# Stacking hi and lo query features in one 128-row operand, and both heads' probabilities through one set of value weights, in the first attention of a two-layer kernel

## The reference, cut to what matters

```python
c_q = hidden_states @ w_q_down                      # 192 latent features
q_nope = c_q @ w_q_up_nope ; q_rope = rope(c_q @ w_q_up_rope)
c_kv = hidden_states @ w_kv_down                    # 64 latents, shared by all heads
q_lat = einsum('bhsd,hdr->bhsr', q_nope, wuk)       # 64 wide
scores = (q_lat . c_kv + q_rope . k_rope) / sqrt(192), causal mask
probs = softmax(scores)
out_lat = einsum('bhst,btr->bhsr', probs, c_kv)     # 64 wide per head
out = einsum('bhsr,hdr->bhsd', out_lat, wuv) ; return out @ w_out
```

## Time and profile before

| | |
|---|---|
| time, median of 3 runs | 2554.64 us (2553.92 to 2555.03) |
| the profiled execution | 2551.88 us, span 2550.0 us |
| PE busy | 2338.2 us, 92% of the span |
| DVE, ACT, POOL busy | 69%, 57%, 62% |
| mean granted TensorE clock | 0.959 of 2.4 GHz |

### The profile page before, as it was taken

How to read it: one execution, slowest core, us unless ns; L and a number is a source line. 1 busy time by engine, 2 the same in 40 slices (tenths; PEclk the granted TensorE clock), 3 DMA queues, 4 the chain that set the end, 5 groups by cost and what they waited for, 6 DMA issues and landing times. The chain is left out here.

```text
span 2550.0 us, 44356 instructions
## 1 busy us (share of the span) xinstructions
PE 2338.2 (92%) x14245; PEld 2027.7 (80%) x14245; DVE 1770.5 (69%) x3131; ACT 1459.0 (57%) x3978; POOL 1572.4 (62%) x1320
## 2 busy tenths in 40 slices
PE   7999999983899889999999999999999999987998
PEld 5788888872588778888888888888888888875886
DVE  4666666666823379888888888888888888972232
ACT  2666656660133347766666666676676766664432
POOL 3555555620154377877887878878878878751442
PEclk8999999995599999999999999999999999998999
DMA  2101110101000120110111111101101111003000
GB/s 97 32 28 36 28 36 23 29 1 41 1 1 1 35 67 29 52 54 16 56 45 37 52 38 48 51 19 57 50 24 56 37 47 48 18 5 141 1 17 17
DMA packets 41349, 93.70 MB, mean 37 GB/s; under 512 B 4836, under 2 KB 6760, under 8 KB 39808
## 3 DMA queue, kind: packets, MB, share of 16 engines
q1 hardware_dynamic: 41092, 90.55, 11.1%
HBM read 79.78 MB, written 10.75 MB: 36 GB/s over the span
## 5 line engine op out<-in xcount | busy, mean ns | idle before, releaser
L1129 POOL TENSOR_TENSOR a_nf_acc<-a_nf_acc,a_nf_term 128x512 f32<-128x512 f32 (+1 forms) x416 | 591.3, 1421 | 140.5 <-ACT a_nf_term L1223 70.1
L1609 POOL TENSOR_TENSOR f_w_lo<-WGU,f_w_hi 128x512 fp32r<-128x512 f32 x88 | 114.8, 1307 | 345.4 <-ACT f_w_hi L1625 345.2
L1183 ACT ACTIVATE a_probs<-bank,a_dip 128x128 f32<-128x128 f32 (+1 forms) x512 | 208.3, 419 | 191.5 <-DVE a_dip L1464 191.5
L1192 ACT ACTIVATE a_probs<-a_probs,a_share 128x128 f32<-128x128 f32 (+1 forms) x512 | 192.5, 464 | 68.7 <-DVE a_share L1470 68.7
L1110 POOL TENSOR_TENSOR a_qk_lo<-a_straight,a_qk_hi 128x512 fp32r<-128x512 f32 (+1 forms) x160 | 194.4, 1217 | 41.2 <-ACT a_qk_hi L1169 41.2
L63 PE MATMUL bank<-a_wo_hi,a_ot_hi 128*128 128x512 f32 x512 | 212.3, 415 | 0.0
L1475 DVE TENSOR_TENSOR a_pt_lo<-bank,a_pt_hi 128x384 fp32r<-128x384 f32 x256 | 140.8, 550 | 90.7 <-ACT a_pt_hi L1200 90.0
L1534 DVE TENSOR_SCALAR a_nf_term<-a_nf_unit 128x512 f32<-128x512 f32 (+1 forms) x288 | 199.7, 738 | 3.4 <-DVE a_nf_unit L1517 0.8
L65 PE MATMUL bank<-a_wo_hi,a_ot_lo 128*128 128x512 f32 x512 | 201.2, 393 | 0.0
L64 PE MATMUL bank<-a_wo_lo,a_ot_hi 128*128 128x512 f32 x512 | 200.8, 392 | 0.0
L1169 ACT ACTIVATE a_qk_hi<-a_straight 128x512 fp32r<-128x512 f32 (+1 forms) x160 | 94.4, 590 | 183.2 <-DVE a_straight L1449 183.2
(11 more groups left out here) (243 smaller groups left out, 8537.1 us busy)
## 6 DMA issues: line engine op xcount, KB each, us to landing
a_raw<-in_l_o SPq DMA_DIRECT2D x64, 256.0 KB, 2.7
a_raw<-in_l_vk SPq DMA_DIRECT2D x32, 384.0 KB, 3.1
a_raw<-in_l_ql SPq DMA_DIRECT2D x32, 320.0 KB, 2.9
a_raw<-in_l_ou SPq DMA_DIRECT2D x32, 288.0 KB, 2.8
n_codes<-coded_w SPq DMA_DIRECT2D x8, 1056.0 KB, 12.8
a_raw<-in_l_nr SPq DMA_DIRECT2D x16, 384.0 KB, 3.1
a_nf_raw<-in_w_nf SPq DMA_DIRECT2D x24, 256.0 KB, 2.6
coded_w<-a_nf_acc SPq DMA_DIRECT2D x24, 256.0 KB, 2.0
```

The lines of the kernel that those rows point to most:

```text
L1129: pool.tensor_tensor(acc, left, nf_term[:, i % CODE_RING, 0:w], ALU.add).then_inc(nf_added, 1)
L1183: act.activation(probs[:, n % 2, col:col + keys], bank[:, at:at + keys], ACT.Exp, bias=dip[:, n % 2, i:i + 1], accum_out=total[:, n % 2, i ...
L1192: ins = act.activation(cell, cell, ACT.Copy, scale=share[:, n % 2, i:i + 1])
L1609: pool.tensor_tensor(lo, src, hi.bitcast(F32), ALU.subtract).then_inc(part_lo[i], 1)
```

## The change

Three things are done together. (1) The 64 features left over: `QW_both[:, i, h, 1, :]` holds their hi weights in rows 0 to 63 and their lo weights in rows 64 to 127, and `CQ.hi[:, 1]` holds the hi latents twice, so one matmul of 128 rows gives hi*hi + lo*hi; a second one, against `CQ.lo` with zeros below, gives hi*lo. Two matmuls of 128 rows stand where three of 64 rows were. (2) `CV` has no zeros any more: `apply` puts both heads' probabilities side by side as 512 (or 2 x 128) moving columns through the same 64 columns of values, into rows 0 to 63 of AV, head 1 in columns 256 to 511. (3) `out_high` and `out_low` bring head 1 down into rows 64 to 127 of OT, with a copy for each head.

```diff
-        QW = pair("qw", [P, PAIRS, NP, 2, P])
+        QW_both, QW_lo = sb("qw_both", [P, PAIRS, NP, 2, P], R32), sb("qw_lo", [P, PAIRS, NP, P], R32)
...
-    return [(x[0][:, i, :, 0, 0:LAT], view[:, 0]), (x[0][0:QP, i, :, 1, 0:LAT], view[0:QP, 1])]
+    return [(QW_both[:, i, :, 0, 0:LAT], QW_lo[:, i, :, 0:LAT], view[:, 0]),
+            (QW_both[0:QP, i, :, 1, 0:LAT], QW_both[QP:P, i, :, 1, 0:LAT], view[0:QP, 1])]
...
 (split_piece, for a piece of kind NR)
+                        tail = both[QP:P, :, 1, :]
+                        pool.tensor_tensor(tail, rope[QP:P, :, 1, :], tail.bitcast(F32), ALU.subtract)\
+                            .then_inc(tail_split, 1)
+                        pool.wait_ge(tail_split, tails[name] + 1)
+                        pool.tensor_tensor(QW_lo[:, i, :, LAT:P], rope[:, :, 0, :], both[:, :, 0, :].bitcast(F32),
+                                           ALU.subtract)
...
 (query_latents_high)
+                    if u // 2 == 1:
+                        ins = act.activation(CQ.hi[QP:P, 1, at], banks[u][0:rows, :], ACT.Copy)
...
 (out_high)
-                    act.activation(OT.hi[:, n % 2, :], AV[:, 0:SEQ], ACT.Copy).then_inc(ot_hi, 1)
+                    for a in range(NP):
+                        ins = act.activation(OT.hi[a * LAT:(a + 1) * LAT, n % 2, :], AV[0:LAT, a * SEQ:(a + 1) * SEQ], ACT.Copy)
+                    ins.then_inc(ot_hi, 1)
...
 (project, unit A)
-                            product(pe, out, QW[:, i, h, 0, :], CQ[:, 0, at], True, False)
-                            last_ = product(pe, out, QW[0:QP, i, h, 1, :], CQ[0:QP, 1, at], False, True)
+                            product(pe, out, (QW_both[:, i, h, 0, :], QW_lo[:, i, h, :]), CQ[:, 0, at], True, False)
+                            pe.matmul(out, QW_both[:, i, h, 1, :], CQ.hi[:, 1, at], start=False, stop=False)
+                            last_ = pe.matmul(out, QW_both[:, i, h, 1, :], CQ.lo[:, 1, at], start=False, stop=True)
...
 (apply)
+                    heads = lambda x: x.rearrange("p (a s) -> p a s", a=NP)
                     for t in range(2):
-                        for a in range(NP):
-                            own = slice(LAT, LAT + P) if a == 0 else slice(0, P)
-                            at = 3 * a * P
-                            last_ = product(pe, AV[:, t * P:SEQ], CV[:, 2 * b + t, own],
-                                            PT[:, at:at + SEQ] if t == 0 else PT[:, at + SEQ:at + 3 * P],
-                                            t == 0 and a == 0, t == 1 and a == NP - 1)
+                        own = tuple(heads(x[:, :])[:, :, t * SEQ:t * SEQ + SEQ - t * P] for x in (PT.hi, PT.lo))
+                        last_ = product(pe, heads(AV[0:LAT, :])[:, :, t * P:SEQ], CV[:, 2 * b + t, :], own, t == 0, t == 1)
...
 (at the start, DVE)
-            for x in (CV.hi, CV.lo):
-                for side in (0, 2):
-                    dve.memset(x[:, :, side * LAT:(side + 1) * LAT].bitcast(F32), 0.0)
+            dve.memset(CQ.lo[QP:P, 1, :].bitcast(F32), 0.0)
...
 (out_low)
-                    dve.tensor_tensor(OT.lo[:, n % 2, :], AV[:, 0:SEQ], OT.hi[:, n % 2, :].bitcast(F32), ALU.subtract)\
-                       .then_inc(ot_lo, 1)
+                    for a in range(NP):
+                        at = slice(a * LAT, (a + 1) * LAT)
+                        ins = dve.tensor_tensor(OT.lo[at, n % 2, :], AV[0:LAT, a * SEQ:(a + 1) * SEQ],
+                                                OT.hi[at, n % 2, :].bitcast(F32), ALU.subtract)
+                    ins.then_inc(ot_lo, 1)
```

More of the change, by code:

```diff
@@ L248, in l0_attention_block @@
         landed = [sem("landed0"), sem("landed1")]
-        split_hi, split = sem("split_hi"), sem("split")
+        split_hi, tail_split, split = sem("split_hi"), sem("tail_split"), sem("split")
         unit_done, ring_free, plain_hi = sem("unit_done"), sem("ring_free"), sem("plain_hi")
@@ L267, in span @@
             lists = {"pieces": lambda f, l: [x for _, x in l0_pieces(f, l)], "units": l0_units,
+                     "tails": lambda f, l: [x for _, x in l0_pieces(f, l) if x[0] == "NR"],
                      "roped": lambda f, l: [u for u in l0_units(f, l) if u[0] == "A"],
@@ L282, in groups, with plain_cells @@
             body(L0_GROUPS - 1, False, True)
-        def plain_cells(name, bank, x):
+        def plain_cells(name, bank):
             i = name[1]
@@ L328, in body @@
                 number, _ = span("units", first, last, g)
+                tails, _ = span("tails", first, last, g)
                 def split_piece(name):
@@ L334, in split_piece @@
                     if kind == "NR":
-                        cells = [(lambda x: x[0][:, i % 2, :, :].rearrange("p h n -> p (h n)"), 0, 2 * (QL + LAT)),
-                                 (lambda x: x[1][:, i, :, :, LAT:P].rearrange("p h k r -> p (h k) r"),
-                                  2 * (QL + LAT), 4 * ROPE)]
+                        wide, rope = raw[:, slot, 0:2 * (QL + LAT)], raw[:, slot, 2 * (QL + LAT):768]\
+                            .rearrange("p (h k r) -> p h k r", h=NP, k=2)
+                        hi, lo = (x[:, i % 2, :, :].rearrange("p h n -> p (h n)") for x in (WN.hi, WN.lo))
+                        both = QW_both[:, i, :, :, LAT:P]
+                        cells = [(hi, lo, wide), (both, None, rope)]
                         user = ("W", i - 2, ahead) if i >= 2 else ("A", L0_STEPS - PAIRS + i)
@@ L345, in split_piece @@
                     hold(pool, passed["pool"], (landed[slot], 8 * (index - slot) + 16), (unit_done, free))
[L346 to L350, removed]
-                        pool.tensor_scalar(hi, src, 1.0, 1.0, ALU.mult, ALU.mult).then_inc(split_hi, 1)
[L352 to L358, removed]
+                    for hi, _, src in cells:
+                        pool.tensor_scalar(hi, src, 1.0, 1.0, ALU.mult, ALU.mult).then_inc(split_hi, 1)
+                    pool.wait_ge(split_hi, 2 * index + 2)
+                    if kind == "NR":
+                        tail = both[QP:P, :, 1, :]
[4 more added lines that the diff above has]
+                                           ALU.subtract)
+                        cells = cells[0:1]
+                    for hi, lo, src in cells:
                         ins = pool.tensor_tensor(lo, src, hi.bitcast(F32), ALU.subtract)
@@ L404, in query_latents_high @@
                     act.wait_ge(lat_done, u + 1)
-                    act.activation(lat_dst[u // 2]((CQ.hi, KC.hi), slice(h * HALF, (h + 1) * HALF)), banks[u][0:rows, :],
-                                   ACT.Copy).then_inc(lat_hi, 1)
+                    at = slice(h * HALF, (h + 1) * HALF)
+                    ins = act.activation(lat_dst[u // 2]((CQ.hi, KC.hi), at), banks[u][0:rows, :], ACT.Copy)
+                    if u // 2 == 1:
+                        ins = act.activation(CQ.hi[QP:P, 1, at], banks[u][0:rows, :], ACT.Copy)
+                    ins.then_inc(lat_hi, 1)
             def key_latents_high():
@@ L416, in value_latents_high @@
                 act.wait_ge(lat_done, 7)
-                act.activation(CV.hi[:, :, LAT:2 * LAT], banks[0][:, :].rearrange("p (t r) -> p t r", t=TT), ACT.Copy)\
+                act.activation(CV.hi[:, :, :], banks[0][:, :].rearrange("p (t r) -> p t r", t=TT), ACT.Copy)\
                    .then_inc(lat_hi, 1)
@@ L431, in plain_high @@
                     act.wait_ge(unit_done, number[name] + 1)
-                    for to, src in plain_cells(name, ring[place[name] % 2], (QW.hi, BH.hi)):
+                    for to, _, src in plain_cells(name, ring[place[name] % 2]):
                         ins = act.activation(to, src, ACT.Copy)
@@ L728, in key_value_latents_low @@
                 dve.wait_ge(lat_hi, 7)
-                dve.tensor_tensor(CV.lo[:, :, LAT:2 * LAT], banks[0][:, :].rearrange("p (t r) -> p t r", t=TT),
-                                  CV.hi[:, :, LAT:2 * LAT].bitcast(F32), ALU.subtract).then_inc(lat_ready, 1)
+                dve.tensor_tensor(CV.lo[:, :, :], banks[0][:, :].rearrange("p (t r) -> p t r", t=TT),
+                                  CV.hi[:, :, :].bitcast(F32), ALU.subtract).then_inc(lat_ready, 1)
             def body(g, first, last):
@@ L755, in plain_low @@
                     bank = ring[place[name] % 2]
-                    for (to, src), (high, _) in zip(plain_cells(name, bank, (QW.lo, BH.lo)),
-                                                    plain_cells(name, bank, (QW.hi, BH.hi))):
+                    for high, to, src in plain_cells(name, bank):
                         ins = dve.tensor_tensor(to, src, high.bitcast(F32), ALU.subtract)
@@ L1984, in laid_out @@
     rope[0:QL] = inputs["L0_attn_w_q_up_rope"].reshape(QL, HEADS, ROPE)
+    rope[QL:] = rope[P:QL]
     rope = rope.reshape(2, P, HEADS // 2, 2, ROPE).transpose(2, 1, 3, 0, 4).reshape(HEADS // 2, P, -1)
```

7 lines of the change are left out of this document (4 added, 3 removed).

## The result

The changed kernel takes 2518.3 us as a median of 4 runs (2516.6 to 2521.0), against 2554.3 before (2550.1 to 2555.0): ratio 0.9863, 95% interval 0.9846 to 0.988. The forecast was 2515 in a range of 2499 to 2536, with 92% on faster. The profiled execution took 2520.98 us (span 2519.0), 30.9 less than the one before.

A forecast was written before the change was run, and what follows sets the result against it. PE's work or the rotation's wait for unit A set the step; afterwards a_pt_lo's chain would, at 6.56 us. Gains 42.6 + 2.5 + 3.2 + 1.5 less 4.2, 5.2, 0.5 made 39.9 us: 2512 profiled, 2515 median, range 2499 to 2536.

The forecast's parts named there:

- What bounds before, and the chain behind it: First attention: PE's work sets 7.29 us steps, the rotation 7.37; behind PE, the chain through ACT and DVE to a_pt_lo.
- The new step, 6.56: Plain step of the first attention: a_pt_lo at 5.64, plus 0.62 and 0.30, makes 6.56 us; PE's work 6.03.
- a_ot_hi twice, 0.26 + 0.26: ACT's two copies ahead of a_pt_hi: each taken to hold ACT 0.26 us, as the 128x256 copy does.
- the dear copy: Rival, 13%: ACT's second copy, into other rows, costs 0.54 instead of 0.26; step 6.84, 17 us lost, 2532.
- The sign I had set for being wrong: On ACT in the new profile: distance of the two a_ot_hi copies above 0.4 us.
- The step behind the loop's way back: The 13.21 us step after the loop's jump, mostly at 1.2 GHz: claimed to gain 2.5 us.
- The two falls of the clock after the statistics steps: Last group: PE rests of 2.6 us drop the clock to 1.2 GHz, 2.6 us each, 5.2 lost.
- The two steps with statistics: Two add_output steps of the last group that also carry statistics: DVE's before and after, gaining nothing.
- Start: First steps of the kernel: unit A at 1.2 GHz gains 3.2 us, steps 2 and 3 together 1.5.
- add_output: DVE work in every fourth step delays the next a_dip: 6 steps lose 0.7 us each, 4.2 in all.
- PE keeps the pace: Rival, 7%: the full 1.26 to 1.34 us of each step is gained, 75 us, giving 2480.
- The clock: Rival, 4%: PE's 0.5 us rest per step makes the clock fall repeatedly; slower, 2590 if in half of all steps.

The follow-up runs named there:

- stack only: Changed kernel with only the stacked leftover query features; `apply`, zeros in the values and single copies as in the kernel before: 2502.6 us, ratio 0.9807.
- the two swaps: Kernel before, with ACT's `out_high` moved behind the first head's `probs_high` and DVE's first `probs_low` ahead of `shares`: 2550.6 us, ratio 0.9995.
- the repeat: The changed kernel itself, unaltered, measured once more beside runs of the kernel before: 2513.5 us, ratio 0.9848.
- stack only with late release: Stacked query features only, `apply` and copies as before; `out_high` behind first `probs_high`, DVE's wait for its rotation behind first a_pt_lo: 2493.7 us, ratio 0.9765.

## Why the prediction was right

- **What bounds before, and the chain behind it.** Right. Unit A was given as 1.19 and took 1.19; `apply` 1.08 and 1.04. PE's work was given as 6.03; its record is busy for 6.12, by the starts it needs 5.95 (6.79 less the 0.84 to spare). That the step would not follow PE but a_pt_lo was shown by PE's rest of 0.67 and by stack only, faster with more work for PE. One reading was a little off: the 7.29 us steps of groups 0 and 3 do not hang on PE alone, since with the two swaps the same PE program takes 7.22.
- **The new step, 6.56.** Measured 6.79 to 6.80, outside the 6.5 to 6.65 to which the forecast gave 72%. The term that was mis-sized is ACT's: a_ot_hi twice, 0.26 + 0.26, measured 0.79. Every other piece held: 2.97 to the first exponential, 1.60 for the exponentials, 0.52 to a_pt_lo, 0.61 to the second `turn`, 0.30, sum 6.79. I had taken the row of the 128x256 copy as the lower bound because "the trace has no 64-row copy into other rows", and named the dear copy a rival at 13% with 0.54 for the second; it costs 0.53 more than a single one. The step without unit A shows the same, 0.51 longer. So this rival came in as to its size, but its step of 6.84 stood for 17 us lost: 0.24 times 56 steps is 13. The sign I had set for being wrong, copies more than 0.4 apart, was just missed: they start 0.39 apart.
- **What made up for it.** The step behind the loop's way back: I left the rest of 2.63 in and put the step at 2.5 less. The rest is gone, 11.19 and 13.21 us became 8.00 and 8.33, and of the 8.1 us only 3.3 had been counted. The two falls of the clock after the statistics steps came, behind rests of 2.77 us each, but lasted 3.4 us each and cost 1.2 and 1.1 (7.99 and 7.89 in place of 6.80) where I had 2.6 each. They are not sure to come: in the repeat PE rests 2.77 and 2.76 at the same two places, and the granted clock fell behind the first and stayed 1.00 behind the second. The two steps with statistics, which I had gain nothing, got 0.36 longer.
- **Start.** 4.7 forecast, 2.1 measured at the start of step 4 (94.56 to 92.45); 0.9 of the difference is the input's landing, that far later in this execution, and the clock fell once more at 82 us.
- **add_output**, 0.7 forecast: plain steps behind it take 7.38 instead of 6.80, 0.6.
- **Rivals.** PE keeps the pace: out, PE rests in every step. The clock: the granted clock is 1.00 in the plain steps with rests of 0.67, as in the step of the earlier trace rows. The rule on short rests that the prediction took from the Trainium skill ("TensorE: Matmul & The Clock Gate", the section on PSUM-queue depth-cycling) is not borne out here: a rest in every step, and over the plain steps of group 2 (331 to 387 us) the granted clock stayed 1.00. The rule on draining from the Trainium skill ("TensorEngine Tiling (Array Packing)", Key Properties) did not show for 64 columns either, while the trace of before shows what the change of rows in unit A had cost.

The total was nearly met, and that is in part luck. The profiled executions lie 30.9 us apart where 39.9 were forecast. Up to the last scores 32.5 were gained: the step took 13 from the forecast and the start 2.6, while the way back gave 4.8 more than counted, the falls 2.9 and add_output 0.7. The medians lie 36 us apart, since the profiled execution of the changed kernel is the slowest of its four, and so 2518 came within some 3 us of 2515. What the runs bear out is the chain that holds the step, not the sum.

## What to carry to other kernels

When an engine is full, look for the step in which it happens not to be: its length is the next bound, and only so much of a saving counts. A copy added to spare matmuls belongs behind what the full engine waits for, not ahead of it; moved by one place, the same work took 2496.9 us instead of 2518.3 (2513.5 in the repeat). Judge what an engine has to spare by the starts of its instructions: here the busy record hid 0.17 us of waiting in each step. And test the halves of a change alone: one half gave all of the gain; the other was slower by itself and gave nothing beside the first as long as the chain held the step above what PE needs without it.

## What was not expected of the hardware

- On ACT a copy that reads rows 0 to 63 and writes rows 64 to 127, between instructions that write from row 0 on, overlaps neither the one ahead of it nor the one behind it: starts 0.39 to 0.40 apart, against 0.26 and 0.27 with the same shape written to rows 0 to 63. Whether the shift does it, or the change of the first row written, was not tried.
- PE paused for 2.5 to 3.0 us at the loop's way back where a pass of the loop has 779 to 876 matmuls, and not at all with 748, whether it had slack within the steps or not. By what the limit is set was not tried.
- The clock's falls did not go by the length of PE's rest alone: in stack only with late release the granted clock fell behind rests of 1.89 and 1.91 us (0.53 over 460 to 463 us, 0.50 over 487.5 to 490), in stack only it stayed 1.00 behind rests of 2.09 and 2.08.
